# A two-layer AdaLN transformer on one core: value scaling one place later on POOL, loops over two rows, norms in halves, gates in weights, the fourth inversion filled

## The reference

```python
h = _layernorm(x, axis=-1) * (1 + ca) + sa
x = x + ga * _L0_attn_ref(h, ...)     # 16 heads of 8, causal softmax
h = _layernorm(x, axis=-1) * (1 + cb) + sb
x = x + gb * _L0_ffn_ref(h, ...)      # 8 experts, top 2, relu
...
h = _layernorm(x, axis=-1) * (1 + ca) + sa
x = x + ga * _L1_attn_ref(h, ...)     # gated delta rule, 12 heads, below
h = _layernorm(x, axis=-1) * (1 + cb) + sb
x = x + gb * _L1_ffn_ref(h, ...)      # gelu
```

```python
S = S * jnp.exp(gt)[..., None, None]
kv = jnp.einsum('bhk,bhkv->bhv', kt, S)
delta = (vt - kv) * bt[..., None]
S = S + jnp.einsum('bhk,bhv->bhkv', kt, delta)
ot = jnp.einsum('bhk,bhkv->bhv', qt, S)
```

## Time and profile before

| | us |
|---|---|
| median of 3 runs | 2684.84 |
| lowest, highest | 2684.17, 2687.9 |
| profiled execution, its own time | 2688.77 |
| span of the profiled execution, first to last instruction | 2687.0 |
| TensorE busy | 2363.3 (88%) |
| VectorE busy | 1786.6 (66%) |
| ScalarE busy | 1426.0 (53%) |
| POOL busy | 813.1 (30%) |

### The profile page before, as it was taken

The page is one execution under the profiler, slowest core; times in us unless marked ns, Lnnn a source line. Parts: engine busy times, 40 slices in busy tenths (PEclk is TensorE's granted clock), DMA queues, the critical chain, the costliest instruction groups (busy, mean ns, idle before and its releaser), DMA issues.

```text
span 2687.0 us, 64860 instructions
## 1 busy us (share of the span) xinstructions
PE 2363.3 (88%) x23706; PEld 1640.8 (61%) x23915; DVE 1786.6 (66%) x4593; ACT 1426.0 (53%) x3033; POOL 813.1 (30%) x573
## 2 busy tenths in 40 slices
PE   3898988999888998989989899898988989889898
PEld 2456765567654775547755477555774567645676
DVE  3458874678637876377754787558865578646786
ACT  0466544754447554385533855447544575446654
POOL 3036310452105421055200642015420253203621
PEclk7899999999999999999999999999999999999999
DMA  8201132011310103101130012300132011320113
GB/s 275 95 1 22 17 100 81 4 20 17 108 72 4 24 13 108 72 9 21 32 137 22 13 20 56 128 5 14 19 105 82 1 19 20 99 81 1 22 17 104
DMA packets 226985, 138.31 MB, mean 51 GB/s; under 512 B 173567, under 2 KB 209799, under 8 KB 219431
## 3 DMA queue, kind: packets, MB, share of 16 engines
q1 hardware_dynamic: 208870, 125.48, 16.4%
q10 hardware_dynamic: 17780, 8.39, 1.1%
HBM read 95.10 MB, written 38.71 MB: 50 GB/s over the span
## 4 chain that ended last, share of the span: by engine, by line
PE 43%; DVE 17%; ACT 16%; issue 9%; DMA 6%; POOL 5%; SPq 3%; ACTq 1%; POOLq 0%; DVEq 0%
PE bank L917 6%; PE bank L698 4%; PE bank L508 3%; PE bank L689 3%; PE bank L621 3%; DVE small L1376 3%; ACT arena L1654 3%; ACT arena L1653 3%; PE bank L546 2%; ACT vq L1661 2%; DVE mx L1181 2%; DVE blk_tx L1378 2%; DMA vq<-k_rows 2%; SPq L2020 2%; PE bank L601 2%
## 5 line engine op out<-in xcount | busy, mean ns | idle before, releaser
L1941 POOL TENSOR_TENSOR arena<-upto,gk 128x1536 f32<-128x1536 f32 x32 | 88.1, 2753 | 684.3 <-DVE beta L1317 684.3
L1324 DVE SCALAR_TENSOR_TENSOR arena<-bank,conv,arena 128x510 f32<-128x510 f32 x320 | 237.1, 747 | 44.8 <-ACT arena L1654 27.1
L508 PE MATMUL bank<-mask_k,ident_bf 128*128 128x512 bf16 x848 | 222.3, 390 | 17.6 <-issue 16.1
L1181 DVE TENSOR_REDUCE mx<-bank 128x2 f32<-128x768 f32 (+3 forms) x187 | 201.6, 1123 | 48.3 <-PE bank L547 47.1
L1933 POOL TENSOR_TENSOR arena<-arena 128x511 f32<-128x511 f32 x160 | 201.6, 1271 | 56.8 <-DVE arena L1324 56.8
L1617 ACT ACTIVATE arena<-bank 128x384 f32<-128x384 f32 (+1 forms) x384 | 168.8, 546 | 49.6 <-PE bank L606 49.5
L759 PE MATMUL bank<-h_pad,arena 128*128 128x512 f32 x320 | 165.6, 615 | 28.5 <-DVE arena L1324 21.7
L546 PE MATMUL bank<-vq 128*128 128x128 bf16 (+3 forms) x528 | 118.6, 310 | 59.7 <-issue 33.2
L1376 DVE TENSOR_TENSOR small<-blk_tx,blk 96x1 f32<-96x1 f32 (+14 forms) x480 | 142.8, 298 | 16.5
L1638 ACT ACTIVATE arena<-bank,b1e 128x512 f32<-128x512 f32 x128 | 87.8, 686 | 116.8 <-PE bank L689 111.7
L1286 DVE SCALAR_TENSOR_TENSOR arena<-bank,comb,arena 128x128 f32<-128x128 f32 x256 | 72.1, 344 | 114.8 <-PE bank L698 113.7
(11 more groups left out here) (303 smaller groups left out, 5850.2 us busy)
## 6 DMA issues: line engine op xcount, KB each, us to landing
vq<-q_rows SPq DMA_DIRECT2D x18, 1024.0 KB, 8.0
vq<-k_rows SPq DMA_DIRECT2D x18, 1024.0 KB, 10.9
arena<-w_bounce SPq DMA_DIRECT2D x16, 1024.0 KB, 6.2
q_rows<-qkp SPq DMA_DIRECT2D x81, 128.0 KB, 2.4
k_rows<-qkp SPq DMA_DIRECT2D x81, 128.0 KB, 2.4
arena<-wv_rows SPq DMA_DIRECT2D x8, 768.0 KB, 10.3
ogt<-wv_rows SPq DMA_DIRECT2D x8, 768.0 KB, 11.7
t_bounce<-blk_tx SPq DMA_DIRECT2D x32, 192.0 KB, 2.1
```

The source lines that it names most:

```text
L508: mm(PS[bank][:, :], ident_bf[:, :], mask_k[:, :, :].rearrange("p h w -> p (h w)"), start=True, stop=True)
L1181: V.reduce_max(dst, unit_scores(u), AX.X).then_inc(s_max, 1)
L1324: ins = V.scalar_tensor_tensor(a[:, k:T], ps[:, 0:T - k], conv[:, n, 3 - k:4 - k], a[:, k:T], ALU.mult, ALU.add)
```

## The change

Five things change together.

- *Loops over two rows.* TensorE, VectorE and ScalarE run NB // 2 turns with two rows written out in each. POOL and SP keep one row a turn. `at` takes a pair (turn, row in it).
- *Norms in halves.* `normalise` signals after two of its four parts, TensorE transposes two and two into two banks, `modulate` works on 256 columns at a time. Fill matmuls around norms fall from 22, 24 and 4 to 19, 18 and 2.
- *Gates in weights.* POOL multiplies the first layer's gates into wproj, b2e and, when it has landed, w2t. VectorE adds the projection directly, and accumulates the experts in xs, so three of its operations on 128 x 512 go.
- *Stages.* On POOL scale_v(1), (2) and (3) move behind one or more other stages each, scale_v(2) with a new wait for ot_ready; gate_keys(3) is left out, and with it the copy of keys for chunk 3 on ScalarE. On VectorE project(0), project(1) and rms(1) change places. On ScalarE rms(1) comes before gate(1), and gate(2) goes behind the fourth inversion, where one pair of table loads serves gate(2) and gate(3).
- *Inversions filled.* In the third, one gate group goes behind the first step, and the fill matmuls get a bank of their own and are four more. In the fourth, project(1) in two parts and the three groups of gate(2) stand between the steps, and there is no fill. Its wait for the projection before is gone; some banks are given out anew.

The diff, without changes of indentation, cut to its core:

```diff
 def at(b, signal, k, ahead=0):
...
+    if isinstance(b, tuple):
+        pair, i = b
+        return pair * (2 * n) + ((i + ahead) * n + k)
+    return b * n + ahead * n + k
...
+def row_of(b, ahead=0):
...
+    pair, i = b
+    return pair * 2 + (i + ahead)
...
-        ln_bank = PS[0]
+        def ln_banks(k):
+            return PS[0], PS[1] if k in ENTER else PS[6]
...
         def qk2_banks(c):
-            return few_banks if c < 2 else PS[3:6]
+            return few_banks if c < 2 else PS[3:6] if c == 2 else [PS[4], PS[5], PS[6]]
...
         def wo_bank(c):
-            return [PS[6], PS[6], PS[1], PS[0]][c]
+            return [PS[3], PS[6], PS[1], PS[0]][c]
...
         def gate_banks(c):
-            return [[PS[7], PS[6], PS[2]], [PS[7], PS[2], PS[6]], [PS[2], PS[7], PS[6]], [PS[3], PS[6], PS[7]]][c]
+            return [[PS[7], PS[6], PS[2]], [PS[7], PS[2], PS[6]], [PS[2], PS[7], PS[3]], [PS[4], PS[5], PS[6]]][c]
...
-                      ("outputs", 1), ("turn_out", 0), ("gram", 3), ("project", 0), ("attend", 3), ("gate_first", 1), ("gate", 1)]
+                      ("outputs", 1), ("turn_out", 0), ("gram", 3), ("project", 0), ("attend", 3), ("gate_first", 1)]
...
-                      ("outputs", 2), ("turn_out", 1), ("gate_first", 2), ("project", 1), ("gate", 2)]
-        pe_stages += [("levels", 3), ("enter_norm", 1), ("gate_first", 3), ("gate", 3), ("enter_qkv", 1),
+                      ("outputs", 2), ("turn_out", 1)]
+        pe_stages += [("levels", 3), ("enter_norm", 1), ("gate", 3), ("enter_qkv", 1),
...
-        act_stages += [("gate", 1), ("rms", 1), ("levels", 2), ("query_part", 2), ("unknowns", 2), ("project", 1)]
-        act_stages += [("gate", 2), ("levels", 3), ("rms", 2), ("enter_norm", 1), ("enter_h", 1), ("gate", 3),
+        act_stages += [("rms", 1), ("gate", 1), ("levels", 2), ("query_part", 2), ("unknowns", 2), ("project", 1)]
+        act_stages += [("levels", 3), ("rms", 2), ("gate", 2), ("gate", 3),
...
-                       ("outputs", 1), ("gram", 3), ("project", 0), ("attend", 3), ("rms", 1)]
-        dve_stages += [("levels", 2), ("subst", 3), ("differences", 2), ("scale", 1), ("outputs", 2), ("project", 1)]
-        dve_stages += [("levels", 3), ("enter_stats", 1), ("rms", 2), ("enter_norm", 1), ("enter_h", 1), ("scale", 2), ("enter_qkv", 1),
+                       ("outputs", 1), ("gram", 3), ("rms", 1), ("attend", 3)]
+        dve_stages += [("levels", 2), ("project", 0), ("subst", 3), ("differences", 2), ("scale", 1), ("outputs", 2)]
+        dve_stages += [("levels", 3), ("enter_stats", 1), ("project", 1), ("rms", 2), ("enter_norm", 1), ("enter_h", 1), ("scale", 2), ("enter_qkv", 1),
...
-        pool_stages += [("levels", 0), ("scale_v", 0), ("scale_queries", 0), ("scale_v", 1), ("scale_decays", 2),
-                        ("scale_queries", 1), ("gate_keys", 2), ("mask", 3), ("scale_v", 2), ("rms", 0)]
-        pool_stages += [("decay_state", 1), ("scale_decays", 3), ("rms", 1), ("gate_keys", 3), ("scale_v", 3)]
-        pool_stages += [("decay_state", 2), ("rms", 2), ("enter_qkv", 1), ("enter_q", 1), ("enter_k", 1)]
+        pool_stages += [("levels", 0), ("scale_v", 0), ("scale_queries", 0), ("scale_decays", 2),
+                        ("scale_queries", 1), ("gate_keys", 2), ("mask", 3), ("scale_v", 1), ("rms", 0)]
+        pool_stages += [("decay_state", 1), ("scale_decays", 3), ("rms", 1), ("scale_v", 2)]
+        pool_stages += [("decay_state", 2), ("rms", 2), ("scale_v", 3), ("enter_qkv", 1), ("enter_q", 1), ("enter_k", 1)]
...
             def transpose_norm(b, k):
-                pe.wait_ge(ln_xn, at(b, ln_xn, k + 1))
...
-                    last = tr(ln_bank[:, t * P:(t + 1) * P], xn[:, t, :], ident[:, :])
+                    if t % 2 == 0:
+                        pe.wait_ge(ln_xn, at(b, ln_xn, 2 * k + t // 2 + 1))
+                    last = tr(ln_banks(k)[t // 2][:, t * P:(t + 1) * P], xn[:, t, :], ident[:, :])
+                    if t % 2:
...
-            with pe.Fori(0, NB) as b:
+            with pe.Fori(0, NB // 2) as pair:
+                for i_row in range(2):
+                    b = (pair, i_row)
...
                 def layer_norm(k):
-                    bank, n = {1: (7, 22), 2: (5, 24), LEAVE: (7, 2)}[k]
+                    bank, n = {1: (7, 19), 2: (5, 18), LEAVE: (7, 2)}[k]
...
-                    keep_warm(bank, 4)
-                    pe.wait_ge(h_ready, at(b, h_ready, k + 1))
+                    keep_warm(bank, 2)
+                    pe.wait_ge(h_ready, at(b, h_ready, 2 * k + 2))
...
+                pe.wait_ge(wp_gated, at(b, wp_gated, 1))
...
-                    last = mm(ps[:, t * D:(t + 1) * D], y_t[:, t * P:(t + 1) * P], wproj[:, :], start=True, stop=True)
+                    last = mm(ps[:, t * D:(t + 1) * D], y_t[:, t * P:(t + 1) * P], wproj_g[:, :], start=True, stop=True)
...
+                pe.wait_ge(w2_gated, at(b, w2_gated, 1))
...
-                    last = mm(ps[:, t * D:(t + 1) * D], comb_t[0:NE, t * P:(t + 1) * P], b2e[:, :], start=True, stop=True)
+                    last = mm(ps[:, t * D:(t + 1) * D], comb_t[0:NE, t * P:(t + 1) * P], b2e_g[:, :], start=True, stop=True)
...
-                        pe.wait_ge(wo_done, at(b, wo_done, c - 1))
...
+                        if c < 2:
                         keep_warm(3, {3: 4, 4: 2, 6: 2}.get(s, 0))
+                        elif c == 2:
+                            if s == 1:
+                                gate_group(1, 2)
+                            elif s == 3:
+                                pe.wait_ge(gate_ready, at(b, gate_ready, NG + 1))
+                            keep_warm(7, {3: 4, 4: 3, 6: 3, 7: 2}.get(s, 0))
+                        elif c == 3 and s in (1, 3):
+                            project(1, range(0, 4) if s == 1 else range(4, HD))
+                        elif c == 3 and s in (4, 6, 7):
+                            gate_group(2, (4, 6, 7).index(s))
...
                 def gate_first(c):
...
-                    elif c == 2:
-                        pe.wait_ge(o_ready, at(b, o_ready, NG * (c + 1)))
-                    elif c + 1 == NT:
-                        pe.wait_ge(wo_done, at(b, wo_done, c - 1))
...
+                    if c == 1:
+                        pe.wait_ge(gd_ready, at(b, gd_ready, NG * NT))
+                        gate_group(c, 1)
...
                 def gate_proj(c):
...
-                    elif c + 1 < NT:
-                        if c == 1:
-                            pe.wait_ge(gd_ready, at(b, gd_ready, NG * (c + 3)))
-                        gate_group(c, 1)
-                        pe.wait_ge(wo_done, at(b, wo_done, c))
-                        gate_group(c, 2)
...
-                        pe.wait_ge(gate_ready, at(b, gate_ready, NG * c))
+                        pe.wait_ge(lv_sb, at(b, lv_sb, L_SB * NT))
+                        gate_group(c, 0)
...
+                        pe.wait_ge(wo_done, at(b, wo_done, 2))
...
                 def unknowns(c):
...
+                    if c == 2:
+                        pe.wait_ge(wo_done, at(b, wo_done, 1))
...
-                def project(c):
+                def project(c, lot=range(HD)):
...
+                    if lot.start == 0:
...
-                    for h in range(HD):
+                    for h in lot:
...
+                    if lot.stop == HD:
...
             def normalise(b, k, src):
...
+                    if t % 2:
...
             def modulate(b, k, dst, mod):
-                dve.wait_ge(ln_ps, at(b, ln_ps, k + 1))
-                V.tensor_scalar(dst, ln_bank[:, :], mod[:, 1:2], mod[:, 0:1], ALU.mult, ALU.add).then_inc(h_ready, 1)
+                for i in range(2):
+                    half = slice(T // 2 * i, T // 2 * (i + 1))
+                    dve.wait_ge(ln_ps, at(b, ln_ps, 2 * k + i + 1))
+                    V.tensor_scalar(dst[:, half], ln_banks(k)[i][:, half], mod[:, 1:2], mod[:, 0:1], ALU.mult, ALU.add).then_inc(h_ready, 1)
...
-            with dve.Fori(0, NB) as b:
...
+            with dve.Fori(0, NB // 2) as pair:
+                for i_row in range(2):
+                    b = (pair, i_row)
...
-                def gate_row(i):
-                    return gates[:, i, :].unsqueeze(1).to_broadcast([P, NT, D])
...
-                V.tensor_tensor(wide_t, tiles(proj_bank), gate_row(0), ALU.mult).then_inc(dve_step, 1)
-                dve.wait_ge(dve_step, step())
...
-                V.tensor_tensor(xs[:, :, :], xin[:, :, :], wide_t, ALU.add).then_inc(xin_free, 1)
+                V.tensor_tensor(xs[:, :, :], tiles(proj_bank), xin[:, :, :], ALU.add).then_inc(xin_free, 1)
...
-                V.tensor_copy(moe, tiles(b2_bank)).then_inc(dve_step, 1)
+                V.tensor_tensor(xs[:, :, :], tiles(b2_bank), xs[:, :, :], ALU.add).then_inc(dve_step, 1)
...
-                        last = V.scalar_tensor_tensor(moe[:, t, :], moe_bank(e)[:, t * D:(t + 1) * D], comb[:, t, e:e + 1],
```

(24 more changed lines are left out.)

## The result

The changed kernel took 2641.89 us (median of 4 runs, 2631.52 to 2644.91) where the kernel before took 2685.1 in the same comparison: ratio 0.9823, 95% interval 0.9805 to 0.984. It is faster by 1.8%, 43 us. Forecast were 2635 us and a gain of 49.6 us.

A forecast was written before the change was run, and what follows sets the result against it. No single engine bounds the kernel but a relay between engines in each row. Terms of 5.2 us a row, 41.6 us over eight, plus 8 us for boundaries make 49.6 us: from 2684.84 to 2635 us, range 2618 to 2658.

The forecast's parts named there:

- Boundaries, 2.0 us a turn: Between rows: unrolling two rows removes four pauses at the loop's turn, 2.0 us each, 8 us, bounds 3 and 10.
- Rival 3: Loop turns: the pause is no price of the loop, only 41.6 us count, 2643 us; chance 0.12.
- Gates, 2.1 us a row: VectorE at the residual norms: gates in the weights save 0.7 us at the first and 1.4 us at the second.
- The cover: Before the experts: POOL's scaling of w2t, taken as 3.6 us, is done about 23 us before its product is needed.
- Halves, 0.6 us a norm: Both residual norms: working in halves shortens the way from last normalisation to modulation by 0.6 us, bounds 0.3 to 0.7.
- rival 1: Row end and norms: the row end eats its gain and halves cost their dear bound, 2652 us; chance 0.15.
- GpSimd, 0.6 us a row: POOL's order: scaling values later moves the first chunk's squares up, sparing VectorE's wait for them, 0.6 us a row.
- Rival 5: POOL's new scaling place: it meets another two-input instruction, the earlier squares are lost, 5 us less, 2640 us; chance 0.05.
- Rival 2: VectorE's port stall at L1346 was on the path, paying 2.5 us a row, 20 us more, 2615 us; chance 0.08.
- Third inversion, 0.4 us a row: Third inversion: second level starts 1.2 us earlier, four more fill matmuls give back 0.8, net gain 0.4 us a row.
- Fourth inversion and row end, 0.8 us: Filled fourth inversion ends 2.3 us earlier, gates behind it cost 1.57; gain 0.8 us a row, bounds -0.7 and 1.8.
- Rival 4: Fourth inversion: filled, it starts no earlier, +5.7 us a row where -0.8 was taken, 2687 us, not faster; chance 0.05.

The follow-up runs named there:

- eight-row kernel: Changed kernel with all eight rows written out in one turn of the loop, so no turn inside the work: 2616.9 us, ratio 0.9763 to the kernel before.

## Why the prediction was right, and where it was not

- **Boundaries, 2.0 us a turn.** Alone, on the kernel before, four turns gave 9.4 us: right. In the changed kernel the same four were worth 25.4. What I mis-sized is the step "2.0 each, 8 us for four, bounds 3 and 10": its bounds held the pause and the lowered clock right behind it, and not the stops and falls inside the rows, which change with the turns and with the body. The way of the maxima was also 1.2 us shorter than summed. Rival 3, that the pause is no price of the loop, falls; so does the 51 ns of the Trainium skill ("Advanced Engine Details and Errata", Control Flow Timing) as the price of a turn here: the runs measured 2.3 us on the kernel before, 1.4 at the low end of the interval.
- **Gates, 2.1 us a row.** Right: 2.1 by the two stretches, 2.0 by the clean row. The cover held although w2t's product was longer.
- **Halves, 0.6 us a norm.** Mis-sized: 0.38 and 0.49, so 0.9 us a row where 1.2 were forecast, and 0.7 by the clean row. From the last normalisation (436.40 + 1.12 = 437.52) to the end of the modulation (437.71 + 0.99 = 438.70) it takes 1.18 us, not the 0.97 of the working, for 1.56 before. A gain of 0.38 is near the dear bound of 0.3 that rival 1 has.
- **GpSimd, 0.6 us a row.** The term that was furthest off: 1.9. The wait for the squares was priced rightly; with the old places it is 7.1 us in 8 rows against 0.9, which is 0.8 us a row. What the term put at nothing is a second collision of the old order, in the third inversion: 1.1 us a row, and the kernel before had it as well, on another instruction (L1480, 2.10 us for 0.29). Rival 5 had this the wrong way round: the collision waits at the old place, not at the new one. Rival 2's 20 us did not come. Its stall, the 2.68 us of L1346, is not on the path: in the second row it comes back with the old places (L1371, 565.77), and L1383 starts 572.95 - 564.55 = 8.40 us behind L1369, where it is 569.19 - 560.84 = 8.35 without it. A stall of its kind is, some 50 us later in the row.
- **Third inversion, 0.4 us a row.** Wrong in sign: it costs 0.6 us a row by the stretch, 1.1 by the clean row. The failed step is "so the second level starts 1.2 us earlier": the idle time of 1.13 us was GpSimd's scaling on VectorE's addition, and is gone where the scaling is moved and VectorE's order is as before. The medians are the same.
- **Fourth inversion and row end, 0.8 us.** The mechanism ran as written: start behind the transposes, 16.3 us (16.8 forecast), q 6.6 us behind the end against 5.2. The working has a slip: by its own prices the eight filling products are 0.81 + 5 x 0.22 = 1.9 us and not 1.7, so 16.6. Measured: 1.1 by the medians, 1.3 from transposes to q against the kernel before and 1.5 to 2.0 with this part alone taken out, 2.1 by the clean row. Rival 4 falls, and rival 1 in its first half; its dear halves nearly came.
- **The sum.** 5.2 us a row and 8 for the turns were forecast. The two traces give 49 in the rows and 11 between them, less 1.9 at the start and 0.8 for the clock. By the medians it is 43 to 48, since the changed kernel's other executions had a lower clock than the profiled one; the kernel before kept 0.982 to 0.989. Parts came out over and under, and falls of the clock, which I had counted only at the boundaries, took the excess back. That the sum lands so near is in part luck: a term three times too small, one of the wrong sign and losses that were not in the sum offset each other. The parts taken out one by one cost 86 us in sum, for a gain of 48. In clean rows they sum to 2.0 + 0.7 + 1.9 + 2.1 - 1.1 = 5.6 us, near the 6.2; the excess of the medians lies in the turns and in the clock. The gating of the keys that the change leaves out (gate_keys(3)) and the new banks stand in every changed kernel and were not taken apart.
- **The signs.** The product on w2t ends well ahead of the experts, and q comes 1.26 us earlier in every row. One sign of being wrong did show: in row three the clock is at the lower level from 751.2 to 754.6, over the projection and the fill of the first norm. The kernel before has this in four rows, so it speaks of no price of the change.

## What to carry to other kernels

Before costing a part, take the time that is lost to the granted clock out of every row, and compare what is left: medians of kernels with many small stops mix the edit with the luck of its falls. When a loop with a long body turns, look for the price both at the turn and further on, at the first dense run of short instructions. An "idle, released by nothing" of one microsecond inside such a run was absent here once a few long instructions stood ahead of it; look whether a packet of an instruction queue starts just before it. And when an idle time is to be filled, ask first which instruction made the engine late: here it was a 0.29 us addition that took 2.10 us beside GpSimd, and moving GpSimd's work was the cure.

## What the runs showed of the hardware

- TensorE stopped for 0.6 to 1.24 us, with no releaser, within runs of 32x32 and 64x64 products in the inversions, at a few places of the row that change from kernel to kernel. All 39 such stops of the 14 traces end 2.2 to 2.9 us behind the start of a packet of the instruction queue q8; the pauses at 45 turns end 2.6 to 3.2 us behind one. That late instructions are the cause fits this, and the fewer packets of the instruction queue with fewer turns; it is argued, not shown. Why the kernel before, with the same products and as many packets as the changed one with loops over one row (128 on q14), stops only at its turns is open.
- The eight-row kernel has other stops as well: 0.62 us at the state product L979 in each row, and 0.66 to 1.29 us at the row's scores in three, where TensorE goes on 3.7 to 15.6 us behind the start of the last packet of q8, and with no fall of the clock right behind any.
- A VectorE instruction of 0.17 us took 2.68 and 1.39 us, and one of 0.29 us took 2.10, each ending within 0.15 us of the end of a GpSimd instruction on 128x1536 or 128x768.
- Falls of the clock cost 1.7 us each or a multiple (3.4, 5.1). In the traces of the kernel before, the changed kernel (both), loops over one row and no turn, nearly each of the 9 to 26 falls in the rows of a trace followed an idle time of TensorE of 0.67 to 3.2 us, but a trace has 119 to 162 such idle times, most are followed by none, and what decides between them is open. A fall of 1.7 us late in the row stands in some rows 284 to 288 us into it, in others at 300 to 304 or 314 to 325; no run tells why.
- The first row begins at 80.6 us before and at 81.4 to 84.3 in the other kernels; no run tells why.
